# The value matmuls of half a group of heads: sixteen in one stretch instead of four times four

## The reference, cut to what matters

```python
scores = einsum('bhnd,bhld->bhnl', q, k) * inv_sqrt_d + mask[:, None]
attn = softmax(scores, axis=-1)
o = einsum('bhnl,bhld->bhnd', attn, v)
```

## Time and profile before

| | |
|---|---|
| median of 3 runs | 1081.67 us (1077.81 to 1084.91) |
| the profiled execution, its own time | 1082.19 us |
| its span, first to last instruction | 1080.4 us |
| PE busy | 945.7 us (88%) |
| DVE busy | 784.5 us (73%) |
| ACT busy | 552.2 us (51%) |
| value matmuls, line 1321, busy | 80.1 us (x1024) |
| mean granted clock of TensorE | 0.958 of full speed |

### The profile page before, as it was taken

One profiled execution on the slowest core, in us unless ns is written; L12 is line 12 of the kernel. 1 busy time (PEld: TensorE's weight loads), 2 busy tenths in 40 slices (PEclk: granted clock), 3 DMA queues, 4 the chain that ended last, 5 costly groups with the idle time before them and its releaser, 6 DMA issues.

```text
span 1080.4 us, 16212 instructions
## 1 busy us (share of the span) xinstructions
PE 945.7 (88%) x5784; PEld 612.5 (57%) x5784; DVE 784.5 (73%) x1975; ACT 552.2 (51%) x1104; POOL 91.5 (8%) x68
## 2 busy tenths in 40 slices
PE   3999879999999978569989989999999999899557
PEld 2777767767767654356644456644556544566223
DVE  5887863351616059579979899798899798899565
ACT  3444312221212147359944679835689537699243
POOL 4444100000000000000012000031000040000100
PEclk9999989999999998879999999999999999999869
DMA  6331400010203066861017820019610148400001
GB/s 214 117 117 39 156 1 1 34 45 1 79 1 117 1 216 242 185 156 41 2 40 156 189 85 2 24 36 190 165 57 2 40 87 176 127 2 2 1 0 39
DMA packets 45888, 86.00 MB, mean 80 GB/s; under 512 B 7408, under 2 KB 7408, under 8 KB 44784
## 3 DMA queue, kind: packets, MB, share of 16 engines
q1 hardware_dynamic: 42448, 80.24, 26.5%
q0 software_dynamic: 576, 4.19, 1.1%
q10 hardware_dynamic: 2784, 0.54, 0.3%
HBM read 43.01 MB, written 8.39 MB: 48 GB/s over the span
## 4 chain that ended last, share of the span: by engine, by line
PE 30%; DVE 17%; issue 5%; ACT 4%; SPq 3%; DMA 3%; POOL 0%; POOLq 0%; DVEq 0%; ACTq 0%
PE psum L1304 9%; PE psum L1321 6%; PE psum L1279 6%; PE psum L1373 3%; SPq L959 3%; DMA k<-k_lo 2%; PE psum L1347 1%; DVE xn L1508 1%; PE psum L1330 1%; DVE amax L1524 1%; DVE hact L1654 1%; DVE qx L1513 1%; DMA x_in<-x_mid_dram 1%; PE psum L1272 1%; DVE stats L49 1%
## 5 line engine op out<-in xcount | busy, mean ns | idle before, releaser
L1106 ACT ACTIVATE probs<-psum,neg_max 128x512 f32<-128x512 f32 x256 | 174.6, 690 | 27.6 <-DVE neg_max L1586 27.6
L1586 DVE CUSTOM_DVE_ANT_0 psum<-psum,m_in 128x512 f32<-128x512 f32 x256 | 174.8, 701 | 11.0 <-issue 8.2
L1304 PE MATMUL psum<-ident,probs 128*128 128x128 f32 x1024 | 154.8, 275 | 0.0
L1304 PEld LDWEIGHTS psum<-ident,probs 128*128 128x128 f32 x1024 | 127.7, 141 | 21.6 <-issue 4.0
L1279 PE MATMUL psum<-k,q 128*128 128x512 f32 x256 | 125.0, 493 | 11.3 <-ACT probs L1106 7.9
L496 PE MATMUL psum<-w_sb,hT 128*128 128x512 f32 x256 | 115.1, 593 | 0.0
L380 ACT ACTIVATE hT<-psum,b_col 128x256 f32<-128x256 f32 x64 | 26.9, 471 | 136.3 <-PE psum L416 136.3
L937 POOL TENSOR_TENSOR xres<-xres,xn 128x512 f32<-128x512 f32 x16 | 19.8, 1275 | 844.8 <-DVE xn L1697 844.8
L1612 DVE COPY probsT<-psum 128x512 f32<-128x512 f32 x128 | 87.9, 686 | 2.7 <-PE psum L1304 2.5
L1097 ACT COPY probsT<-psum 128x512 f32<-128x512 f32 x128 | 74.9, 585 | 23.2 <-PE psum L1304 21.0
L414 PE MATMUL psum<-xselT_hi,w_hi 128*128 128x256 f32 x256 | 82.9, 324 | 4.2 <-ACT onehotT L374 4.2
(11 more groups left out here) (209 smaller groups left out, 1733.6 us busy)
## 6 DMA issues: line engine op xcount, KB each, us to landing
c_in<-in_ctx_dram SPq DMA_DIRECT2D x8, 1024.0 KB, 5.1
bw_in<-in_L_ffn_W_dram SPq DMA_DIRECT2D x8, 1024.0 KB, 11.2
k<-k_hi SPq DMA_DIRECT2D x32, 256.0 KB, 6.4
k<-k_lo SPq DMA_DIRECT2D x32, 256.0 KB, 7.6
q<-q_hi SPq DMA_DIRECT2D x64, 128.0 KB, 2.4
q<-q_lo SPq DMA_DIRECT2D x64, 128.0 KB, 2.3
xres<-in_x_dram SPq DMA_DIRECT2D x4, 1024.0 KB, 4.9
w_raw<-in_L_ffn_w_dram POOLq DMA_DIRECT2D x4, 1024.0 KB, 5.1
```

Of the source, the lines that this page charges most:

```text
L1106: act.activation(probs[:, u % 4, :], psum[u % SCORE_BANKS][:, :], ACT.Exp, scale=-1.0, bias=neg_max[:, u:u + 1], accum_out=prob_sum[:, nt, ...
L1304: mm = pe.transpose(turn_bank(u)[:, l * P:(l + 1) * P], probs[:, u % 4, l * P:(l + 1) * P], ident[:, :])
L1586: dve.tensor_tensor_reduce(bank[:, :], bank[:, :], m_in[:, nt, :], -1.0, LOWEST, ALU.add, ALU.min, neg_max[:, u:u + 1]).then_inc(masked_re ...
```

## The change

The four groups of four value matmuls, at i = 0, 2, 4 and 6, become one stretch of sixteen at i = 0 (AV_STEPS = 8, so only i = 0 is due, and the inner loop runs over all four l). What they wait for, the banks, the order over l and r, and the release of `av_psum` after the last one stay as they are. `av_psum` is now raised in step 11 + 8 hg instead of 17 + 8 hg.

```diff
@@ -890,6 +890,7 @@
         STACKS = HPG * 4
+        AV_STEPS = 8
@@ -1305,8 +1306,7 @@
                         hg, i = divmod(s - LAG - UH, UH)
-                        if 0 <= hg < HG and i % 2 == 0:
-                            l = i // 2
+                        if 0 <= hg < HG and i % AV_STEPS == 0:
                             if i == 0:
@@ -1316,11 +1316,12 @@
-                            for r in range(HPG):
-                                h = (hg // 2) * HPG + r
-                                mm = pe.matmul(psum[6 + hg % 2][HD * r:HD * (r + 1), 0:HALF],
-                                               vv[:, l, h * HD:(h + 1) * HD],
-                                               probsT[:, (hg + 1) % 2, r, l, :], start=(l == 0), stop=(l == T - 1))
+                            for l in range(T * i // UH, T * (i + AV_STEPS) // UH):
+                                for r in range(HPG):
+                                    h = (hg // 2) * HPG + r
+                                    mm = pe.matmul(psum[6 + hg % 2][HD * r:HD * (r + 1), 0:HALF],
+                                                   vv[:, l, h * HD:(h + 1) * HD],
+                                                   probsT[:, (hg + 1) % 2, r, l, :], start=(l == 0), stop=(l == T - 1))
                             if l == T - 1:
                                 mm.then_inc(av_psum, 1)
```

## The result

| | before | after |
|---|---|---|
| median | 1081.67 us (1077.81 to 1084.91, 5 runs) | 1091.47 us (1090.0 to 1096.14, 5 runs) |
| ratio | | 1.0103 (95% interval 1.0079 to 1.0127) |
| profiled execution, its own time | 1082.19 us | 1096.14 us |
| middle half group | 8.79 us | 9.38 us |

(Three runs of the kernel before were named above; over all five the median is the same.) The change makes the kernel slower by 1%. The time forecast was 1096.6; the median came out 5 us lower, inside the range. The profiled execution of the changed kernel happens to be the slowest of its five, so its span (1094.4 us) overstates the change. That its own time, 1096.14, all but meets the forecast of 1096.6 is luck.

What follows compares the result with a forecast made beforehand. PE's list, with one small wait, was taken as the bound (8.79 us a half group). A hole in the scores was to make it 9.57, +3.61 us a batch, four batches +14.4: 1082.2 + 14.4 = 1096.6 us, range 1086 to 1103.

Steps and rivals of the forecast that it cites:

- one small wait: On PE, a half group's first value block starts 0.69 us after its transposes, not 0.52, waiting for ACT's copy.
- switch pair: On PE, going into the narrow shape and out costs 0.28 us; three fewer save 0.84 us a half group.
- The hole: In the attention, the next score waits behind the stretch, so DVE stands still 1.29 us, from 3.90 to 5.19.
- The rest of the period on DVE: DVE from mask s+1 to mask s+5: 4.42 us, giving a half group of 9.54 to 9.61, taken as 9.57.
- the scaling: On DVE, the distance over the scaling to mask s+3: 1.12 us, with up to 0.07 of waiting for PE.
- The check of the prices: DVE's share of the forecast period, 9.61 - 1.29 = 8.32 us, set against its recorded 8.26 busy.
- PE's busy time: In a middle half group of the changed kernel, PE's busy time should be down to about 7.8 us.
- The first stretch: At step 11, beside DVE's four `xres` operations, PE has 1.9 us to spare: costed at nothing, window stays at 10.1.
- The sum: Per batch: +4.83 us up to the last mask operation, +3.61 after the tail; four batches +14.4 us.
- The tail: At the end of a batch, -0.71 us from the last value block of half group 6 and -0.51 from the last stretch.
- PE's saving is had: Rival: PE falls to 7.96 us a half group, DVE's 8.26 becomes the bound, 1064.6 us; chance 0.08.
- The clock: Rival: idle PE lets the granted clock fall to 1.2 GHz in the attention, kernel over 1150 us; chance 0.03.

Runs made afterwards that it cites:

- the repeat: The changed kernel run once more with no edit, beside the kernel before: median 1094.06 us against 1082.4, ratio 1.0108.

## Why the prediction was right, step by step

- *PE is the bound before, with one small wait.* Right. Moving the four groups by a step took the wait away, and the half group came to 8.66 against the 8.63 of PE's steps.
- *A switch pair costs 0.28 us, a round 0.215.* Right in size. The stretch of eight rounds took 1.86 us to the next score (676.89 to 678.75), as forecast. The 0.28 is what a block costs beyond its rounds; no run parts the change of shape in it from whatever else a block costs. That it is saved three times is true, and of no use there.
- *The hole.* Right to a few hundredths. With the mask of unit s-3 at 0 (674.08) the forecast had ACT's exps at 0.79 and 1.46, its copy at 2.13, the stretch at 2.81, the next score at 4.67 and its mask at 5.19. Measured: 0.79, 1.47, 2.13, 2.81, 4.67 and 5.22.
- *The rest of the period on DVE.* **The step that failed.** The prediction gave it 4.42 us; it took 9.38 - 5.22 = 4.16. I had read DVE's prices from start to start in the kernel before, mask to mask 0.67 and copy to mask 0.66, as if they were its own pace. They held waits: the mask operation at 668.94 starts 0.52 us after its score at 668.42, which is exactly the distance that I had listed as score to mask. DVE's own distances are 0.62 and 0.61 (mask to copy is 0.65, not 0.62). That part is some 0.08 of the 0.26. The larger part, 0.18, is the scaling: 1.12 forecast and 0.94 measured (680.65 to 681.59). In the kernel before it held a wait for the transposes of the finished half group, and I had allowed for 0.07. The gap was then 1.47 from start to start (5.22 less 3.75) and not 1.29, but the period shorter: 9.38 instead of 9.57.
- *The check of the prices.* The sum of 8.32 against DVE's 8.26 busy looked like a confirmation and wasn't. An operation of DVE is recorded for 0.69 us and the next starts 0.61 us after it, so up to 0.08 us of waiting hides under the record of the operation before. Busy time there is an upper bound of the need: 7.99 of it was enough in the changed kernel.
- *PE's busy time.* Forecast 7.8, recorded 8.39, for the same reason. The forecast is what its steps add up to (8.80 - 0.17 - 0.84 = 7.79). The records hold waits as well: between the scores at 674.51 and 675.70 are 1.19 us where a step needs 0.70, so 0.49 of waiting, and the row shows 0.27. A window in which PE is busy 8.65 of 8.65 does not by itself show that it never waits; the sum of its steps does.
- *The first stretch is covered by `xres`.* Right: that window stayed at 10.09 us (10.10 in the last batch).
- *The sum.* Up to the last mask operation +4.83 us a batch was forecast; by the starts in the trace of batch 1 it was 0.74 for the second half group, 4 x 0.60 and 0.65 for the last seven units, together 3.8. The tail gave back 1.20 (forecast 1.22). That is 2.6 us for this batch instead of 3.61; the four batches of the repeat give 9.7 instead of 14.4. About 4 of the 4.7 us missed are the DVE term, and the rest is in the first eight units of a batch, which took 0.2 to 0.3 us less in three of the four.
- *The rivals.* That PE's saving is had did not happen in this kernel; the saving is real and, with the later place, is what makes the two stretches of eight faster. The clock stayed at 1.00 in every middle half group. In one of the two profiled executions it left 1.00 in the last stretch of the last batch, at a cost of 1.3 us.

## What to carry to other kernels

When work on one engine is gathered into a longer stretch, ask first what the other engines can do while it lasts. Here DVE has about a microsecond of work in hand when the stretch begins (begun at 2.81, in hand up to 3.75), and a mask can start 0.55 us after its score, so a stretch of 1.86 us starves it, while one of 1.00 us hardly does if it does not begin with a wait. Put such a stretch where all it needs is long done, which can be one step later than the earliest place. And take an engine's own pace from a stretch where it is the one that is waited for.

## What the runs showed of the hardware that I had not expected

- DVE operations of 128x512 follow each other at 0.60 to 0.65 us though each is recorded for 0.69 to 0.73. A wait shorter than the difference leaves no idle time in the profile. PE's rows hide more: 0.22 of 0.49 us of waiting in the changed kernel (674.51 to 675.70).
- Each time PE goes from 128-column to 32-column matmuls and back, 0.28 us is spent beyond the rounds themselves, against 0.215 us for a round of four such instructions side by side. In a half group with four value blocks this is 1.1 of the 2.8 us.
